# Gathering the early sums' pieces into the first step of each group of four tiles, ahead of v on ScalarE

## The chip, the cores and the metric

The kernel runs on one core of a Trainium2 chip. The metric is the time of the whole kernel on the device, in microseconds; the time before is the median of three runs. The engines work side by side and meet at semaphores: TensorE (PE), VectorE (DVE), ScalarE (ACT), GpSimd (POOL), and SyncE (SP), which here only issues transfers. In the trace every engine but PE's weight loads starts its instructions in the order of the program, so one that waits holds back all that stand behind it on its engine.

## What is computed

Sixteen sequences of 512 tokens with 128 features go through a state-space mixer and then through a layer of eight experts, two per token. The reference, cut to the second half:

```
h = _layernorm(x, axis=-1) * (1 + cb) + sb
probs, idx = jax.lax.top_k(softmax(h @ Wr + br), 2)          # two experts a token
h = _layernorm(jax.nn.relu(xt @ W1[e] + b1[e]), g1, be1)     # 512 wide, for each expert e
y = _layernorm(jax.nn.relu(h @ W2[e] + b2[e]), g2, be2)      # 128 wide
out = gate[t, e1] * y[e1, t] + gate[t, e2] * y[e2, t]
x = x + gb * out
```

## The kernel before

First the mixer runs over the 16 sequences ("batches", b), routes every token to two experts and writes the tokens' rows, sorted by expert, to DRAM. Then the expert stage runs over 135 tiles of 128 rows (EXPERT_TILES), each of one expert. It is a software pipeline: `expert_step(s)` is written once for each engine, and in step s an engine works on several tiles at once, for instance PE on the hidden layer of tile s (`hidden`, L1612 to L1614, the first instruction of a step for three tiles in four), the second layer of tile s-4 (L1725) and the transposes of tile s-2 (`turn_hidden`, L1620). A first step of a group of four (s % 4 == 0, TOGETHER = 4) begins on PE with the bias rows of four tiles (L1602).

On ACT a step is, in the order of the program: `high_part` (L799, h3hi), `hidden` (L803, relu into r), v (L906, relu of the second layer's value), `hidden_turned` (L807, the transposed hidden layer into rT), vs (L914), sde (L918, a square root). In a first step `hidden_turned` stands ahead of v; in the others behind it. DVE's step has v0 (`values`, L1398, which empties PE's value bank), the reciprocal (L1406, needs sde of the step before), vg (`scaled`, L1409, which v waits for), h3lo (L1176, which PE's next hidden layer waits for), two statistics and the target rows (L1382). POOL adds a shift to each result (L699) and scatters the rows to DRAM (L711).

The weighted sum of a token's two results is made while the expert stage runs, for the first 11 batches (EARLY). SP loads a batch's results from DRAM into early01 (`load_early`, L596, 512 KB; two buffers, the tile name is xi) and the batch is then taken in four pieces (b, j) of 128 tokens. For a piece, ACT scales the first result (`early_y0g`, L879, into a tile n), DVE adds the second result times its gate (`early_sum`, L1493), POOL multiplies by gb and adds x (L752, L758). 44 pieces are spread evenly over steps 53 to 136:

```
def piece_tile(b, j):
    return FIRST_COMBINED + (b * J + j) * (LAST_PIECE - FIRST_COMBINED) // (EARLY * J - 1)

def early_y0g(b, j):
    if j == 0:
        act.wait_ge(early_loaded[b % 2], b // 2 * 16 + 16)
```

The first piece of batches 0 to 10 falls on steps 53, 60, 68, 76, 83, 91, 99, 107, 114, 122 and 130. SP's loop is a queue of its own, ahead of the engines: its turn i loads the rows of tile i and the shifts of tile i-6, and waits for POOL's add of tile i-14 to free the shifts' buffer. The load of batch b is issued in turn piece_tile(b, 0) + 1 (LOADED_AT), behind that turn's other transfers; in a turn that opens a group of four these are six, since the biases of four tiles go ahead.

Of the kernel before, what the change touches and what calls it, by code (L numbers as in the profile page):

```python
# [6 lines left out]
def adaln_ssm_moe_kernel(nc, x_in, win_in, bin_in, bp_in, cp_in, dp_in, wout_in, bout_in, wr_in, br_in,  # L7
# [24 lines left out]
    J = L // P  # L32
# [10 lines left out]
    EXPERT_TILES = TOPK * NT + E - 1  # L43
# [24 lines left out]
    with ExitStack() as ctx:  # L68
# [51 lines left out]
        TOGETHER = 4  # L120
# [115 lines left out]
        EARLY = EXPERT_TILES // 8 + 1 - EARLY_TURN  # L236
# [12 lines left out]
        def piece_tile(b, j):  # L249

            return FIRST_COMBINED + (b * J + j) * (LAST_PIECE - FIRST_COMBINED) // (EARLY * J - 1)

        def pieces_at(i):

            return [(b, j) for b in range(EARLY) for j in range(J) if piece_tile(b, j) == i]

        assert all(tiles_for(b) + 14 <= piece_tile(b, 0) for b in range(EARLY))
        WIDE_UNTIL = 32
# [47 lines left out]
        def rows_bank(i):  # L306
            s = i - 2
            return bank[7] if s % 2 else hidden_banks[(s // TOGETHER + 1) * TOGETHER % len(hidden_banks)]
# [84 lines left out]
        def on(i, n):  # L393

            return not isinstance(i, int) or 0 <= i < n
# [21 lines left out]
        def norms(s):  # L417

            return slice(0 if on(s - 3, EXPERT_TILES) else 1, 2 if on(s - 6, EXPERT_TILES) else 1)
# [358 lines left out]
        def _(act):  # L778
# [18 lines left out]
            def high_part(i, of):  # L797
                act.wait_ge(t3_done, i + 1)
                nc.scalar.activation(h3hi[i % DEPTH], of, ACT.Copy).then_inc(h3hi_ready, 1)  # L799

            def hidden(i):
                act.wait_ge(h_done, i + 1)
                nc.scalar.activation(r[i % DEPTH], hidden_bank(i)[:], ACT.Relu).then_inc(r_ready, 1)  # L803

            def hidden_turned(i):
                act.wait_ge(tr_done, i + 1)
                nc.scalar.activation(rT[i % DEPTH], turned_bank[:], ACT.Copy).then_inc(rT_ready, 1)  # L807
# [59 lines left out]
            def half_gates():  # L867
                act.wait_ge(lead_ready, 1)
                nc.scalar.activation(gate[:, 0, :], lead[:], ACT.Tanh, scale=0.5).then_inc(half_gate_ready, 1)
                nc.scalar.activation(root_of_eps[:], eps[:], ACT.Sqrt)  # L870

            def early_y0g(b, j):
                if b == 0 and j == 0:
                    act.wait_ge(gates_ready, 1)
                if j == 0:
                    act.wait_ge(early_loaded[b % 2], b // 2 * 16 + 16)
                    if b >= 2:
                        act.wait_ge(early_sum_ready, (b - 1) * J)
                nc.scalar.activation(y0g[b % 2][:, j, :], early01[b % 2][:, j, 0:D], ACT.Copy,  # L879
                                     scale=gate[:, 0, b * J + j:b * J + j + 1]).then_inc(early_y0g_ready, 1)  # L880


            def late_y0g(b, groups):
                if groups[0] == 0:
                    act.wait_ge(late_loaded[b], 16)
                for j in groups:
                    nc.scalar.activation(late01[b][:, j, 0:D], late01[b][:, j, 0:D], ACT.Copy,  # L887
                                         scale=gate[:, 0, b * J + j:b * J + j + 1]).then_inc(early_y0g_ready, 1)

            def expert_step(s, n):  # L890
                q = n % 2
                last_of_group = s % TOGETHER == 0
                if on(s + 1, EXPERT_TILES) and s + 1 >= EARLY_H:
                    high_part(s + 1, rows_bank(s + 1)[:, 0:P])
                if s == 1:
                    half_gates()
                if on(s - 1, EXPERT_TILES) and s - 1 >= EARLY_H:
                    hidden(s - 1)
                turned_first = s >= EXPERT_TILES or last_of_group
                if on(s - 3, EXPERT_TILES) and s > 3 and turned_first:  # L900
                    hidden_turned(s - 3)
                if on(s - 5, EXPERT_TILES):
                    act.wait_ge(v0_ready, s - 4)
                    if on(s - 7, EXPERT_TILES):
                        act.wait_ge(vg_ready, s - 6)
                    nc.scalar.activation(v[1 - q][:], v0[1 - q], ACT.Relu).then_inc(v_ready, 1)  # L906
                if on(s - 3, EXPERT_TILES) and s > 3 and not turned_first:
                    hidden_turned(s - 3)
                if on(s - 8, LAST_SHIFTED):
                    act.wait_ge(vg_ready, s - 7)  # L910
                    act.wait_ge(rse_ready, s - 4)
                    if on(s - 8 - VS, EXPERT_TILES):
                        act.wait_ge(y_ready, s - 7 - VS)
                    nc.scalar.activation(vs[(s - 8) % VS], vg[q][:], ACT.Copy, scale=rse[q][:, 1:2]).then_inc(vs_ready, 1)  # L914
                if on(s - 3, EXPERT_TILES) or on(s - 6, EXPERT_TILES):
                    both = norms(s)
                    act.wait_ge(mve_ready, s - 2)
                    nc.scalar.activation(sde[q][:, both], mve[q][:, both, 1], ACT.Sqrt, bias=eps[:]).then_inc(sde_ready, 1)  # L918
                for b, j in pieces_at(s):
                    early_y0g(b, j)  # L920
                if s == EXPERT_TILES + 3:
                    late_y0g(EARLY, range(HALF))
                if s == EXPERT_TILES + 4:
                    late_y0g(EARLY, range(HALF, J))
# [27 lines left out]
        def _(dve):  # L952
# [471 lines left out]
            def hidden_norm(s, q, p):  # L1424
                dve.wait_ge(stf_ready, s - 2)
                dve.nop(nofuse=True)
                return vec.bn_aggr(mve[q][:, 0, :], stf[p][:])

            def last_step(s, n):
                q, p = n % 2, 1 - n % 2  # L1430
                if on(s - 5, EXPERT_TILES):
                    values(s, q, p)
                if on(s - 3, EXPERT_TILES):
                    hidden_norm(s, q, p)
                if on(s - 2, EXPERT_TILES):
                    hidden_stats(s - 2)
                if on(s - 6, EXPERT_TILES):
                    value_stats(s, q)
                    value_norm(s, q).then_inc(mve_ready, 1)
                reciprocals(s, p)  # L1440
                scaled(s, p)

            def expert_step(s, n):
                if s >= EXPERT_TILES:
                    last_step(s, n)
                    return
                q, p = n % 2, 1 - n % 2
                if s == TABLE2_STEPS + 1:
                    dve.wait_ge(spread_done, 2)
                    dve.wait_ge(y_done, TABLE2_STEPS - 3)  # L1450
                    write_table(bank[5], ROUND1, EXPERT_TILES)
                    dve.wait_ge(table_ready, 2)
                stats_first = s % TOGETHER == 0 and s > TOGETHER
                if stats_first:
                    hidden_norm(s, q, p)
                    hidden_stats(s - 2)
                if on(s - 5, EXPERT_TILES):
                    values(s, q, p)
                if on(s - 4, EXPERT_TILES) or on(s - 7, EXPERT_TILES):
                    reciprocals(s, p)  # L1460
                if on(s - 7, EXPERT_TILES):
                    scaled(s, p)
                if on(s + 1, EXPERT_TILES) and s + 1 >= EARLY_H:
                    low_part(s + 1, rows_bank(s + 1)[:, 0:P])
                if on(s - 6, EXPERT_TILES):
                    value_stats(s, q)
                if on(s - 3, EXPERT_TILES) and not stats_first:
                    ins = hidden_norm(s, q, p)
                if on(s - 2, EXPERT_TILES) and s > 2 and not stats_first:
                    hidden_stats(s - 2)  # L1470
                if on(s - 6, EXPERT_TILES):
                    ins = value_norm(s, q)
                if on(s - 3, EXPERT_TILES) or on(s - 6, EXPERT_TILES):
                    ins.then_inc(mve_ready, 1)
                if on(s, TABLE2_STEPS):
                    round2_table(s)
                if on(s, EXPERT_TILES):
                    target_of(s, n % SLOTS)
                for b, j in pieces_at(s - 1):
                    early_sum(b, j)  # L1480
                if isinstance(s, int) and s == 4:
                    all_gates()
# [23 lines left out]

            run_tiles(expert_step)

            for i in range(EXPERT_TILES - 1, EXPERT_TILES + 2):
                for b, j in pieces_at(i):  # L1510
                    early_sum(b, j)

# [275 lines left out]
```

## Time and profile before

| | us |
|---|---|
| median of three runs | 512.86 (512.68 to 513.87) |
| the profiled execution, its own time | 515.06 |
| its span in the trace | 513.1 |
| PE busy in the span | 487.1 |
| DVE busy | 445.1 |
| ACT busy | 412.6 |

The expert stage takes the stretch from about 175 to 500 us of the span. Times in rows are counted from the span's start; a row of the timeline gives start, duration, engine, line, operation, tiles (the tile written, then an arrow, then those read), and in brackets how long the engine had been idle before it and what ended that. The k-th L1612 of PE belongs to tile k, so the distance of two of them is the length of a step.

### The profile page before, as it was taken

How to read it: one execution, taken by the hardware profiler on the slowest of the kernel's cores; microseconds unless marked ns; L12 is line 12 of the kernel's file. 1: busy time of each engine (PE TensorE's matmuls, PEld its weight loads, DVE VectorE, ACT ScalarE, POOL GpSimd, SP SyncE). 2: the span in 40 equal slices, each digit the busy share in tenths (PEclk: the TensorE clock that was granted, in tenths of full speed). 3: DMA queues.
4: the chain of work that ended last, by engine and by line, in shares of the span. 5: the costliest groups of instructions: out<-in, count | busy, mean ns of one | idle time of the engine just before them, and what ended most of it. 6: DMA issues, size and time to landing. Idle time of an engine off the chain costs nothing. (4 is left out here: it accounts for less than half of the span.)

```text
span 513.1 us, 15015 instructions
## 1 busy us (share of the span) xinstructions
PE 487.1 (95%) x3051; PEld 372.0 (72%) x3051; DVE 445.1 (87%) x2217; ACT 412.6 (80%) x1140; POOL 360.1 (70%) x483
## 2 busy tenths in 40 slices
PE   7989999999987799999999999999999999999994
PEld 6445656555545588888888778888888888888861
DVE  7779999998887599888887789999999999999994
ACT  3679887978764588889888888898888898999984
POOL 1003666666667778888888878788787788988871
PEclk9999999999995699999999999999999999999998
DMA  6980111154111568878726686765766667666665
GB/s 167 309 240 21 46 48 46 48 130 114 52 47 55 135 151 164 161 225 198 178 89 157 178 204 162 191 194 159 208 190 145 192 208 203 175 180 207 189 177 164
DMA packets 80329, 78.36 MB, mean 153 GB/s; under 512 B 11420, under 2 KB 73015, under 8 KB 80242
## 3 DMA queue, kind: packets, MB, share of 16 engines
q1 hardware_dynamic: 71826, 60.48, 46.9%
q0 software_dynamic: 8416, 16.93, 9.3%
q8 instruction: 29, 0.48, 0.4%
q14 instruction: 58, 0.48, 0.3%
HBM read 55.20 MB, written 22.62 MB: 152 GB/s over the span
## 5 line engine op out<-in xcount | busy, mean ns | idle before, releaser
L683 POOL DMA_INDIRECT expert_rows<-rows_ring,slot x128 | 123.3, 964 | 94.5 <-issue 78.4
L711 POOL DMA_INDIRECT expert_results<-y,target x119 | 120.8, 1015 | 30.6 <-issue 24.5
L1725 PE MATMUL bank<-W,h2T 128*128 x720 | 97.4, 278 | 1.8 <-issue 0.8
L1725 PEld LDWEIGHTS bank<-W,h2T 128*128 128x128 f32 x720 | 88.2, 193 | 13.1 <-issue 6.7
L906 ACT ACTIVATE v<-wmod 128x128 f32<-128x128 f32 x135 | 41.8, 310 | 40.0 <-DVE vg L1409 35.0
L1612 PE MATMUL bank<-W1hi,h3hi 128*128 x135 | 66.6, 494 | 1.4 <-DVE h3lo L1176 1.4
L792 ACT ACTIVATE n<-X,nm,rs 128x128 f32<-128x128 f32 x128 | 54.1, 485 | 12.8 <-DVE nm L1343 12.8
L1398 DVE SCALAR_TENSOR_TENSOR wmod<-bank,rse,shifts 128x128 f32<-128x128 f32 x119 | 41.0, 344 | 24.2 <-PE bank L1725 23.3
L1181 DVE BATCH_NORM_STATS2 stf<-h1T 128x6 f32<-128x512 f32 x90 | 59.3, 659 | 0.4 <-ACT h1T L803 0.4
L1620 PE MATMUL bank<-ident_wr,h1T 128*128 128x128 f32 x360 | 55.2, 276 | 0.0
L1613 PE MATMUL bank<-W1lo,h3hi 128*128 x135 | 54.4, 403 | 0.0
L1614 PE MATMUL bank<-W1hi,h3lo 128*128 x135 | 54.2, 401 | 0.0
L803 ACT ACTIVATE h1T<-bank 128x512 f32<-128x512 f32 x90 | 53.0, 589 | 0.6 <-PE bank L1614 0.6
L807 ACT ACTIVATE h2T<-bank 128x512 f32<-128x512 f32 x90 | 52.8, 587 | 0.3 <-PE bank L1620 0.3
L1725 PE MATMUL bank<-W,third_rT 128*128 x360 | 48.1, 276 | 0.9 <-DVE wmod L1398 0.7
L1725 PEld LDWEIGHTS bank<-W,third_rT 128*128 128x128 f32 x360 | 43.7, 191 | 6.0 <-issue 2.3
L1409 DVE SCALAR_TENSOR_TENSOR vg<-v,mve,shifts 128x128 f32<-128x128 f32 x119 | 44.2, 371 | 0.0
L1620 PEld LDWEIGHTS bank<-ident_wr,h1T 128*128 128x128 f32 x360 | 42.7, 143 | 1.2 <-issue 0.4
L918 ACT ACTIVATE sde<-mve,eps 128x2 f32<-128x2 f32 (+1 forms) x138 | 40.7, 295 | 1.7 <-DVE mve L1422 0.7
L1176 DVE TENSOR_TENSOR h3lo<-bank,h3hi 128x128 fp32r<-128x128 f32 x135 | 38.0, 282 | 2.4 <-ACT h3hi L799 2.3
L799 ACT ACTIVATE h3hi<-bank 128x128 fp32r<-128x128 f32 x135 | 34.8, 260 | 4.5 <-PE bank L1593 4.5
L1417 DVE BATCH_NORM_STATS2 sty<-v 128x6 f32<-128x128 f32 x135 | 38.0, 282 | 0.2
(249 smaller groups left out, 1196.9 us busy)
## 6 DMA issues: line engine op xcount, KB each, us to landing
shifts<-expert_shifts SPq DMA_DIRECT2D x119, 192.0 KB
hrow<-expert_rows SPq DMA_DIRECT2D x135, 65.0 KB
xi<-expert_results SPq DMA_DIRECT2D x12, 512.0 KB, 5.2
out_x<-X SPq DMA_DIRECT2D x15, 256.0 KB
X<-in_L_attn_x SPq DMA_DIRECT2D x7, 512.0 KB, 7.4
b_ring<-b_two_parts SPq DMA_DIRECT2D x135, 4.0 KB
W1lo<-in_L_ffn_W SPq DMA_DIRECT2D x4, 512.0 KB, 6.7
expert_rows<-rows_ring,slot POOLq DMA_INDIRECT x128
```

The source lines that it names most:

```text
L683: nc.gpsimd.indirect_dma_start(out=rows_d, out_offset=bass.IndirectOffsetOnAxis(ap=slot[q][:, n // TOPK, n % TOPK:n % TOPK + 1], axis=0), ...
L711: nc.gpsimd.indirect_dma_start(out=results_d, out_offset=bass.IndirectOffsetOnAxis(ap=target[i % TARGETS][:], axis=0), in_=y[k], in_offset ...
L792: ins = nc.scalar.activation(dst[:, j:j + 1, :], X[:, bass.ds(b * J + j, 1), :], ACT.Identity, bias=nm_[:, x_tiles + j:x_tiles + j + 1], s ...
L803: nc.scalar.activation(r[i % DEPTH], hidden_bank(i)[:], ACT.Relu).then_inc(r_ready, 1)
L807: nc.scalar.activation(rT[i % DEPTH], turned_bank[:], ACT.Copy).then_inc(rT_ready, 1)
L1181: vec.bn_stats(stf[i % 2][:], r[i % DEPTH]).then_inc(stf_ready, 1)
L1409: vec.scalar_tensor_tensor(wide(vg[p][:]), wide(v[p][:]), mve[p][:, 1, 0:1], wide(shift_rows[ring(s - 7)][:, D:2 * D]), ALU.subtract, ALU. ...
L1612: mm(h, h3hi[i % DEPTH], W1hi[:, bass.ds(e, 1), :], start=False, stop=False)
L1613: mm(h, h3hi[i % DEPTH], W1lo[:, bass.ds(e, 1), :], start=False, stop=False)
L1614: mm(h, h3lo[i % DEPTH], W1hi[:, bass.ds(e, 1), :], start=False, stop=True).then_inc(h_done, 1)
L1620: ins = tr(turned_bank[:, ch * P:(ch + 1) * P], r[i % DEPTH][:, ch * P:(ch + 1) * P], ident[:])
L1725: ins = mm(acc, rT[(s - 4) % DEPTH][:, ch * P:(ch + 1) * P], W2[:, bass.ds(e4 * CF + ch, 1), :], start=(ch == 0), stop=(ch == CF - 1))
```

## The change

The function that tells which pieces belong to a step now takes piece_tile rounded down to a multiple of four, so that pieces go to the first step of their group: two in most groups, three in step 80, one in step 136. On ACT they stand behind `hidden_turned` and ahead of v, where before a piece stood at the end of its step. On DVE the sum of a piece stands at the end of the same step, where before it stood at the end of the next. The turns in which SP issues loads and stores still go by piece_tile itself.

```
--- before.py
+++ after.py
@@ -252,7 +252,7 @@
 
         def pieces_at(i):
 
-            return [(b, j) for b in range(EARLY) for j in range(J) if piece_tile(b, j) == i]
+            return [(b, j) for b in range(EARLY) for j in range(J) if piece_tile(b, j) // TOGETHER * TOGETHER == i]
 
         assert all(tiles_for(b) + 14 <= piece_tile(b, 0) for b in range(EARLY))
         WIDE_UNTIL = 32
@@ -899,6 +899,8 @@
                 turned_first = s >= EXPERT_TILES or last_of_group
                 if on(s - 3, EXPERT_TILES) and s > 3 and turned_first:
                     hidden_turned(s - 3)
+                for b, j in pieces_at(s):
+                    early_y0g(b, j)
                 if on(s - 5, EXPERT_TILES):
                     act.wait_ge(v0_ready, s - 4)
                     if on(s - 7, EXPERT_TILES):
@@ -916,8 +918,6 @@
                     both = norms(s)
                     act.wait_ge(mve_ready, s - 2)
                     nc.scalar.activation(sde[q][:, both], mve[q][:, both, 1], ACT.Sqrt, bias=eps[:]).then_inc(sde_ready, 1)
-                for b, j in pieces_at(s):
-                    early_y0g(b, j)
                 if s == EXPERT_TILES + 3:
                     late_y0g(EARLY, range(HALF))
                 if s == EXPERT_TILES + 4:
@@ -1476,7 +1476,7 @@
                     round2_table(s)
                 if on(s, EXPERT_TILES):
                     target_of(s, n % SLOTS)
-                for b, j in pieces_at(s - 1):
+                for b, j in pieces_at(s):
                     early_sum(b, j)
                 if isinstance(s, int) and s == 4:
                     all_gates()
@@ -1506,7 +1506,7 @@
 
             run_tiles(expert_step)
 
-            for i in range(EXPERT_TILES - 1, EXPERT_TILES + 2):
+            for i in range(EXPERT_TILES, EXPERT_TILES + 2):
                 for b, j in pieces_at(i):
                     early_sum(b, j)
```

ACT in step 80 of the expert stage; `n_1` and `n_0` are the scaled results of an odd and an even batch (here 3 and 4), and the brackets name the semaphores that a row waits for. Before:

```order
L807 ACTIVATE third_rT<-bank 128x512 [waits tr_done]
L906 ACTIVATE v<-wmod 128x128 [waits vg_ready,v0_ready]
L914 ACTIVATE wmod<-vg,rse 128x128 [waits y_ready,rse_ready,vg_ready]
L918 ACTIVATE sde<-mve,eps 128x2 [waits mve_ready]
L879 ACTIVATE n_1<-xi,gate 128x128
L799 ACTIVATE h3hi<-bank 128x128 [waits t3_done]
```

Now:

```order
L807 ACTIVATE third_rT<-bank 128x512 [waits tr_done]
L879 ACTIVATE n_1<-xi,gate 128x128 x2
L879 ACTIVATE n_0<-xi,gate 128x128 [waits early_sum_ready,early_loaded0]
L908 ACTIVATE v<-wmod 128x128 [waits vg_ready,v0_ready]
L916 ACTIVATE wmod<-vg,rse 128x128 [waits y_ready,rse_ready,vg_ready]
L920 ACTIVATE sde<-mve,eps 128x2 [waits mve_ready]
L799 ACTIVATE h3hi<-bank 128x128 [waits t3_done]
```

The first piece of batch 4, which waits for that batch's load (early_loaded0), has come from the end of step 83 to the middle of step 80, and v, vs, sde and the next step's h3hi stand behind it.

DVE at the end of step 80 and the start of step 81 (target of tile 80, then v0 of the next step). Before:

```order
L1382 TENSOR_SCALAR target<-hrow,tile_e 128x1 [waits result_stored0,hrow_loaded0]
L1398 SCALAR_TENSOR_TENSOR wmod<-bank,rse,shifts 128x128 [waits rse_ready,shifts_loaded4,y_done]
L1406 RECIPROCAL rse<-sde 128x2 [waits vs_ready,sde_ready]
L1409 SCALAR_TENSOR_TENSOR vg<-v,mve,shifts 128x128
L1176 TENSOR_TENSOR h3lo<-bank,h3hi 128x128 [waits h3hi_ready]
```

Now:

```order
L1382 TENSOR_SCALAR target<-hrow,tile_e 128x1 [waits result_stored0,hrow_loaded0]
L1493 SCALAR_TENSOR_TENSOR n_1<-xi,gate,n_1 128x128 [waits early_y0g_ready] x2
L1493 SCALAR_TENSOR_TENSOR n_0<-xi,gate,n_0 128x128 [waits early_gb_ready,early_y0g_ready]
L1398 SCALAR_TENSOR_TENSOR wmod<-bank,rse,shifts 128x128 [waits rse_ready,shifts_loaded4,y_done]
L1406 RECIPROCAL rse<-sde 128x2 [waits vs_ready,sde_ready]
```

Three sums now stand between the targets of step 80 and v0 of step 81, and the third waits for the piece of batch 4 on ACT. PE's and SP's instructions are the same rows in the same order before and now.

## Rows read from the trace of the kernel before

**Rows 1.** The page: busy time by engine, and granted clock in 40 slices

```profile
PE 487.1 (95%) x3051; PEld 372.0 (72%) x3051; DVE 445.1 (87%) x2217; ACT 412.6 (80%) x1140; POOL 360.1 (70%) x483
...
PEclk9999999999995699999999999999999999999998
```

**Rows 2.** Timeline of PE: first hidden matmul of some steps

```profile
294.92 0.48 PE L1612 MATMUL bank<-W1hi,h3hi 128*128 x1
...
310.35 0.50 PE L1612 MATMUL bank<-W1hi,h3hi 128*128 x1
...
319.55 0.50 PE L1612 MATMUL bank<-W1hi,h3hi 128*128 x1
...
356.98 0.50 PE L1612 MATMUL bank<-W1hi,h3hi 128*128 x1
...
359.14 0.48 PE L1612 MATMUL bank<-W1hi,h3hi 128*128 x1
...
378.70 0.48 PE L1612 MATMUL bank<-W1hi,h3hi 128*128 x1
...
398.30 0.48 PE L1612 MATMUL bank<-W1hi,h3hi 128*128 x1
...
417.17 0.47 PE L1612 MATMUL bank<-W1hi,h3hi 128*128 x1
...
424.20 0.50 PE L1612 MATMUL bank<-W1hi,h3hi 128*128 x1
...
454.15 0.47 PE L1612 MATMUL bank<-W1hi,h3hi 128*128 x1
```

**Rows 3.** DMA issues: KB each, median us from issue to landing

```profile
xi<-expert_results SPq DMA_DIRECT2D x12, 512.0 KB, 5.2
```

**Rows 4.** Timeline of SP's queue: loads of batches 0, 4 to 7, 9

```profile
288.80 0.39 SPq L596 DMA_DIRECT2D xi<-expert_results  x1
...
358.49 0.38 SPq L596 DMA_DIRECT2D xi<-expert_results  x1
...
376.51 0.42 SPq L596 DMA_DIRECT2D xi<-expert_results  x1
...
396.05 0.42 SPq L596 DMA_DIRECT2D xi<-expert_results  x1
...
415.36 0.38 SPq L596 DMA_DIRECT2D xi<-expert_results  x1
...
447.89 0.43 SPq L596 DMA_DIRECT2D xi<-expert_results  x1
```

**Rows 5.** Timeline, steps 96 and 97: ACT, DVE and PE

```profile
396.71 0.31 ACT L906 ACTIVATE v<-wmod 128x128 f32<-128x128 f32 x1
...
397.20 0.29 ACT L918 ACTIVATE sde<-mve,eps 128x2 f32<-128x2 f32 x1
...
398.49 0.33 DVE L1409 SCALAR_TENSOR_TENSOR vg<-v,mve,shifts 128x128 f32<-128x128 f32 x1
...
398.92 0.31 ACT L906 ACTIVATE v<-wmod 128x128 f32<-128x128 f32 x1 [0.76 <-DVE vg L1409]
...
399.13 0.58 ACT L807 ACTIVATE h2T<-bank 128x512 f32<-128x512 f32 x1
...
400.09 0.60 PE L1620 MATMUL bank<-ident_wr,decay 128*128 128x128 f32 x4
```

**Rows 6.** Groups by line, 290 to 490 us: busy us, mean ns | idle

```profile
L1493 DVE SCALAR_TENSOR_TENSOR n<-xi,gate,n 128x128 f32<-128x128 f32 x42 | 19.3, 460 | 0.0
...
L879 ACT ACTIVATE n<-xi,gate 128x128 f32<-128x128 f32 x43 | 16.7, 387 | 0.1
```

**Rows 7.** Timeline of PE, end of mixer and first expert steps

```profile
156.78 2.15 PE L1680 MATMUL bank<-ident_wr,h2T 128*128 128x136 f32 x8 [2.85 <-DVE placed L1321]
...
175.32 0.79 PE L1612 MATMUL bank<-W1hi,h3hi 128*128 x1
...
178.83 0.47 PE L1612 MATMUL bank<-W1hi,h3hi 128*128 x1
```

More of the change, by code:

```diff
@@ L253, in pieces_at @@
         def pieces_at(i):
-            return [(b, j) for b in range(EARLY) for j in range(J) if piece_tile(b, j) == i]
+            return [(b, j) for b in range(EARLY) for j in range(J) if piece_tile(b, j) // TOGETHER * TOGETHER == i]
         assert all(tiles_for(b) + 14 <= piece_tile(b, 0) for b in range(EARLY))
@@ L901, in expert_step @@
                     hidden_turned(s - 3)
+                for b, j in pieces_at(s):
+                    early_y0g(b, j)
                 if on(s - 5, EXPERT_TILES):
@@ L918, in expert_step @@
                     nc.scalar.activation(sde[q][:, both], mve[q][:, both, 1], ACT.Sqrt, bias=eps[:]).then_inc(sde_ready, 1)
-                for b, j in pieces_at(s):
-                    early_y0g(b, j)
                 if s == EXPERT_TILES + 3:
@@ L1478, in expert_step @@
                     target_of(s, n % SLOTS)
-                for b, j in pieces_at(s - 1):
+                for b, j in pieces_at(s):
                     early_sum(b, j)
@@ L1507, in _ @@
             run_tiles(expert_step)
-            for i in range(EXPERT_TILES - 1, EXPERT_TILES + 2):
+            for i in range(EXPERT_TILES, EXPERT_TILES + 2):
                 for b, j in pieces_at(i):
```

## Prediction

> **What bounds the kernel now.** I read the page first: PE is busy 95% of the span, ahead of DVE with 87% and ACT with 80% [rows 1]. So the change, which touches no matmul, can help only where PE now waits, and can hurt only where it makes PE wait. The second view is the timeline of PE, cut down to the first hidden matmul of each step: the distance of two such rows is a step, and what is more than the clean length is PE waiting for someone. The reader is to compare two stretches. From step 60 to step 64 a group of four takes 319.55 - 310.35 = 9.20 us. From step 80 to step 108, seven groups take 424.20 - 356.98 = 67.22 us, and seven clean ones would take 64.40 [rows 2]. So PE loses 2.8 us there, which is the stretch where pieces fall on the last step of a group, and ACT's piece at the end of that step holds back the relu and the copy of the group's first step. The third view is SP's own queue: when each batch's load is issued [rows 4], with the time to landing from the list of transfers, 5.2 us [rows 3]. The fourth is the timeline of all engines over a first step and the one behind it, which shows who waits for whom [rows 5].
>
> **What is moved, and what it costs by itself.** Nothing is removed: 44 pieces on ACT at 0.387 us and as many sums on DVE at 0.46 us [rows 6] stay, and so do POOL's two instructions a piece. On ACT two pieces (0.77 us) now stand ahead of v in a first step. Their cover is ACT's spare time in the next step: in step 97 it stood idle 0.76 us until vg was there [rows 5]. So I cost this at nothing; without the cover it would be up to 0.77 us in each of some 20 groups, 15 us. On DVE two sums a group stand behind one another instead of in two steps; DVE has 13% of the span free [rows 1], about 1.2 us of a group of 9.20, so a lag of one sum is made up within the group. Nothing again; without that, up to 0.46 us a group, 9 us. POOL's pairs come in two turns instead of four, and POOL is busy 70% [rows 1]: its results come late by about one piece and SP's loads with them, which I leave out of the sum. What the change is worth where it does as it says: the 2.8 us of steps 80 to 108, no more, since the groups that are clean already stay as they are.
>
> **The wait that it adds.** The first piece of a batch waits for the batch's load. SP issues that load in turn piece_tile + 1, which the change leaves alone, while the piece moves ahead by up to three steps. For batches 4, 5, 6 and 7 the first piece falls on step 83, 91, 99, 107, always the last of a group, so it moves by three: to steps 80, 88, 96, 104. Take batch 6. Issued at 396.05 [rows 4], landed 5.2 us later, at 401.25. The piece's new place is where v stood, 396.71 in step 96 [rows 5]. ACT would stand there for 4.5 us, less 0.39 for the other piece of the step. Behind it on ACT are v, vs, sde and the next step's h3hi, and on DVE the sum of that same piece waits at the end of step 96, with v0 of step 97 behind it; PE's second layer of step 97 waits for that v0, so PE stops in the step behind the first.
>
> How long after the landing (call it T) does PE go on? On ACT: the piece 0.39, then v to the start of sde 0.49 (396.71 to 397.20), sde 0.29. Then DVE's vg 0.33, then 0.10 until ACT's v of the next step starts (398.49 + 0.33 to 398.92), 0.21 from there to the copy into rT (399.13), which takes 0.58: T + 2.39 in all, and only then can PE transpose. In step 97 undisturbed, this transpose began at 400.09, 1.79 us after the step's first matmul at 398.30 [rows 2, 5]. So the loss is T - (start of the step behind the first) + 0.60. The start is in [rows 2], T is issue [rows 4] plus 5.2:
>
> Batch 4: 363.69 - 359.14 + 0.60 = 5.2. Batch 5: 381.71 - 378.70 + 0.60 = 3.6. Batch 6: 401.25 - 398.30 + 0.60 = 3.6. Batch 7: 420.56 - 417.17 + 0.60 = 4.0. Together 16.4 us. If the chain behind the landing costs nothing (the lower bound), it is 13.9.
>
> For the loads of batches 8 to 10 the piece moves by two steps at most, and the one that comes nearest is batch 9: 453.09 - 454.15 + 0.60 is below nothing, so ACT waits and PE does not. Batches 1 to 3 do not move their first piece. Batch 0 moves by one step, from 53 to 52, and step 53 is a long one already, since SP comes late there: 294.00 + 0.60, plus a mean step of 2.30 (a quarter of 9.20), against 294.92, the start of step 54 before [rows 2, 4], gives 2.0 at most and nothing at least, if the load comes sooner than the 5.2 us; I take 1.0.
>
> The gain of 2.8 us does not come in full. A load's turn is tied to POOL's results of about three steps before the piece, so where the steps between get shorter, the piece asks sooner for a load that comes no sooner, and the time turns up in the wait. I take half, 1.4; bounds 0 and 2.8.
>
> **The clock.** PE stands still for 3 to 5 us in each of the four waits. In this trace the granted clock was half of full, 1.2 GHz, in most of the 12th and 13th of the 40 slices counted from 0 [rows 1], around a place where PE had stood for 2.85 us [rows 7]. A step begun at half clock took 178.83 - 175.32 = 3.51 us [rows 7], 1.21 more than the mean 2.30. How long it would stay low after such a wait, no row of the expert stage shows. Bounds: not at all, and two steps after each of the four waits, 9.7 us. I take one step each, 4.8 us, since these waits are longer than the 2.85. The Trainium skill, TensorE: Matmul & The Clock Gate, section "What's actually happening", says that the slow clock is the default state and that only activity releases it. By that rule every one of the four waits pays, and the sum is the one below; this trace agrees as far as its one slow stretch goes.
>
> **The sum.** 16.4 + 1.0 - 1.4 + 4.8 = 20.8 us. On the profiled execution's own 515.06 this gives 535.9; that execution lies 2.2 us above the median of 512.86, so for the median 533.7, 4.1% slower.
>
> **The rivals.**
> - The waits come but the clock stays (PE has work within each wait, the next step's hidden matmuls). Then 20.8 - 4.8 = 16.0, 528.9. For it: the clock was full in slices 14 to 38 [rows 1], although PE lost time in that stretch too. Against it: these waits are longer than what it lost there in any step. Chance 0.22.
> - The waits are half as long, 514.4 to 524, because loads land sooner: SP's turns would have to come about two us earlier against the steps. For it: the waits themselves give SP time. Against it: each load's turn lies after the recovery from the last wait, and its own transfers ahead of it take their time whatever PE does. Chance 0.09.
> - The other side: the load is there when the piece asks. Then the 2.8 us of steps 80 to 108 go and nothing comes for them: 510.1, faster. It decides at one point, whether the load of batch 6 lands before 396.7 rather than at 401.25, and equally for 4, 5 and 7; it would take loads issued 5 us sooner. Against it: SP's rows are the same in the same order. Chance 0.05.
> - The change does nothing that can be measured: small waits (only ACT's, within its spare 0.76 us) and small gains, within 0.3% (1.5 us, about what a measurement of this kernel can tell from no change). It would take waits of about a microsecond where rows give three to five. Chance 0.03.
>
> **How the numbers follow.** The forecast, waits and slow clock, has 0.61. Its own range is 526 to 541: below, the chain at nothing, the gain in full and one slow step for two waits; above, the sum with two slow steps a wait and 2.0 for batch 0. With the rivals, 521 to 541 leaves out the faster case, the unchanged one and most of the half-long waits, and what is above 541. Slower by over 0.3%: 0.61 + 0.22 + 0.09 = 0.92; within 0.3%: 0.03; faster: 0.05.
>
> **What would show it.** In the profile after, ACT's group of v or of pieces gets new idle time that ends with the load from the results (the waits' list names the transfer), some 4 to 6 us each in steps 80, 88, 96 and 104, and PE's steps 81, 89, 97 and 105 are longer by 3 to 5 us, with v0 on DVE as what they wait for. Steps at a group's end elsewhere go back to clean length. The row of granted clock shows new slices under 9 between 355 and 430 us. I am wrong if the first piece of batches 4 to 7 starts right behind the copy into rT, if PE has other work while ACT waits so that the step behind it does not grow, or if the loss sits in DVE's pairs of sums, spread over all groups.

## The result and the profile after

| | us, median (lowest to highest) |
|---|---|
| before | 512.86 (512.39 to 513.94, 5 runs) |
| after | 534.71 (534.22 to 536.15, 5 runs) |
| ratio | 1.0398, 95% interval 1.037 to 1.0426 |

The change makes the kernel 21.85 us slower. The profiled execution of after took 534.56 us, with a span of 532.5, beside 515.06 and 513.1 before, so the two traces differ by 19.4 us in the span: the profiled execution of before lies 2.2 us above its median.

The page of after: busy time by engine, and the granted clock in 40 slices of 13.3 us. These answer to [rows 1].

```profile
PE 491.2 (92%) x3051; PEld 377.1 (71%) x3051; DVE 443.2 (83%) x2217; ACT 413.5 (78%) x1140; POOL 356.5 (67%) x483
...
PEclk9999999999966999999999999998989989999999
```

No engine has more instructions, and ACT and DVE have hardly more work or less (413.5 and 443.2 us here, 412.6 and 445.1 before). The shares fall because the span has grown: the new time is waiting. New slices under 9 stand in places 27, 29 and 32, counted from 0, which are 359 to 373, 386 to 399 and 426 to 439 us.

The waits of after from 280 to 510 us: who waited, for whom, us in total, how often, the longest.

```profile
ACT n L879 <- DMA xi<-expert_results: 23.9, 8, 5.2
...
DVE n L1493 <- ACT n L879: 21.0, 8, 4.8
...
PE bank L1725 <- DVE wmod L1398: 16.8, 9, 4.3
```

Read downwards, the long waits of these lines are four events, each seen from three engines: ACT's piece waits for the load, DVE's sum waits for the piece, and PE's second layer waits for v0 (L1398), which stands behind that sum on DVE. Each is a little shorter on the next engine, since that engine has a little work left before it stops. Of ACT's 23.9 us, 18.7 are the four; the rest is batch 0 (2.33 us) and the loads of batches 8 to 10 (2.9 us together).

The timeline of after around the four places (start, duration, what, and in brackets the idle time before it and who ended it):

```profile
356.87 0.38 SPq L596 DMA_DIRECT2D xi<-expert_results  x1
...
357.68 0.48 PE L1612 MATMUL bank<-W1hi,h3hi 128*128 x1
...
361.70 0.40 ACT L879 ACTIVATE n<-xi,gate 128x128 f32<-128x128 f32 x1 [5.02 <-DMA xi<-expert_results]
...
362.14 0.35 DVE L1493 SCALAR_TENSOR_TENSOR n<-xi,gate,n 128x128 f32<-128x128 f32 x1 [4.70 <-ACT n L879]
...
362.41 0.34 DVE L1398 SCALAR_TENSOR_TENSOR wmod<-bank,rse,shifts 128x128 f32<-128x128 f32 x1
...
363.01 1.90 PE L1725 MATMUL bank<-W,third_rT 128*128 x8 [4.27 <-DVE wmod L1398]
...
364.70 1.06 PE L1620 MATMUL bank<-ident_wr,h1T 128*128 128x128 f32 x4
...
365.42 0.78 PE L1612 MATMUL bank<-W1hi,h3hi 128*128 x1
...
368.11 0.48 PE L1612 MATMUL bank<-W1hi,h3hi 128*128 x1
...
382.37 0.48 PE L1612 MATMUL bank<-W1hi,h3hi 128*128 x1
...
385.35 0.40 ACT L879 ACTIVATE n<-xi,gate 128x128 f32<-128x128 f32 x1 [4.27 <-DMA xi<-expert_results]
...
391.79 0.49 PE L1612 MATMUL bank<-W1hi,h3hi 128*128 x1
...
405.98 0.48 PE L1612 MATMUL bank<-W1hi,h3hi 128*128 x1
...
409.85 0.40 ACT L879 ACTIVATE n<-xi,gate 128x128 f32<-128x128 f32 x1 [5.16 <-DMA xi<-expert_results]
...
416.19 0.48 PE L1612 MATMUL bank<-W1hi,h3hi 128*128 x1
...
430.36 0.47 PE L1612 MATMUL bank<-W1hi,h3hi 128*128 x1
...
433.32 0.40 ACT L879 ACTIVATE n<-xi,gate 128x128 f32<-128x128 f32 x1 [4.25 <-DMA xi<-expert_results]
...
439.76 0.48 PE L1612 MATMUL bank<-W1hi,h3hi 128*128 x1
```

Steps 81 and 82 run from 357.68 to 368.11, 10.43 us; before they took 4.28. PE had done its part of step 81 at 358.7 and then had nothing until 363.01. The pattern comes back three times, and the second, third and fourth can be read from three rows each: the start of the step behind the piece, the piece, and the start two steps on.

The windows of after in two of the four places: the wait, then the stretch behind it (us, busy time by engine, granted clock, DMA share, GB/s).

```profile
357.70:363.00 5.30, 1.04 (x7) 0.59 (x4) 0.79 (x4) 1.30 (x6) 0.31 (x1) 1.00 0.62 202
363.30:366.70 3.40, 3.40 (x15) 3.15 (x15) 3.03 (x15) 3.09 (x10) 2.75 (x4) 0.51 0.38 113
...
406.00:411.10 5.10, 1.04 (x7) 0.59 (x4) 0.75 (x4) 1.25 (x6) 0.27 (x1) 0.99 0.63 194
411.10:414.50 3.40, 3.34 (x14) 3.25 (x15) 2.86 (x15) 2.92 (x9) 1.62 (x3) 0.51 0.34 105
```

PE works for 1.04 us of the 5.3 of the wait, at a granted clock of 1.00, and then for the whole 3.4 us behind it at 0.51, that is nearly all at 1.2 instead of 2.4 GHz. All four places show this and no other between 300 and 490 us does. The third does not show in the page's row of the clock: it lies across the border of slices 30 and 31, so that neither drops below 9.

**The difference by stretch.** Taking the first hidden matmul of each step (L1612) in both traces and subtracting step lengths gives where the time sits, in us against before. The runs of the next section stand beside it. "The eight steps" are 81, 82, 89, 90, 97, 98, 105 and 106.

| kernel | up to step 3 | 3-50 | 51-56 | 57-80 | the eight steps | other steps 81-107 | 108-133 | sum |
|---|---|---|---|---|---|---|---|---|
| after | -1.3 | -0.1 | -0.3 | +0.2 | **+22.2** | -2.3 | +1.2 | +19.6 |
| load_one_turn_sooner | -1.0 | +0.3 | +1.9 | 0.0 | **+3.7** | -2.1 | 0.0 | +2.8 |
| load_three_turns_sooner | -0.7 | +0.1 | +1.9 | -0.1 | **+0.2** | -2.2 | +0.1 | -0.7 |
| round_up | -0.4 | +1.2 | +1.0 | 0.0 | **-0.2** | -1.2 | +0.1 | +0.5 |
| round_up_load0_later | +0.5 | +0.1 | -1.5 | +0.1 | **-0.2** | -2.1 | +0.1 | -2.9 |
| grouping_alone | -1.1 | +1.8 | -0.2 | +1.3 | **+20.7** | -1.2 | +1.1 | +22.3 |
| sum_one_step_later | +0.2 | +0.6 | +2.4 | +1.4 | **+23.1** | -1.3 | +1.3 | +27.8 |
| busy_in_wait | -1.1 | +0.2 | +1.6 | 0.0 | **+22.6** | -2.5 | +0.2 | +21.1 |
| busy_in_wait_12 | -1.2 | -0.1 | -0.2 | -0.1 | **+21.6** | -1.8 | +0.2 | +18.3 |

No piece lies ahead of step 52, so the first two columns are not the change's: they show how far two executions differ there anyway, up to 1.8 us. The change is in the eight steps.

### The profile page after: what moved, and what is told of

It reads as the page before. It is cut to its first block and busy times, and to the rows that moved or that the text cites. A ratio compares the mean times of both kernels' runs of the same rounds, so it can differ in the third digit from the quotient of the medians.

```text
span 532.5 us, 15015 instructions
## 1 busy us (share of the span) xinstructions
PE 491.2 (92%) x3051; PEld 377.1 (71%) x3051; DVE 443.2 (83%) x2217; ACT 413.5 (78%) x1140; POOL 356.5 (67%) x483
## 5 line engine op out<-in xcount | busy, mean ns | idle before, releaser
L1725 PEld LDWEIGHTS bank<-W,h2T 128*128 128x128 f32 x720 | 88.8, 194 | 19.4 <-issue 12.0
L1612 PE MATMUL bank<-W1hi,h3hi 128*128 x135 | 67.9, 503 | 0.7 <-DVE h3lo L1176 0.7
L1398 DVE SCALAR_TENSOR_TENSOR wmod<-bank,rse,shifts 128x128 f32<-128x128 f32 x119 | 41.1, 345 | 24.8 <-PE bank L1725 21.7
L1725 PE MATMUL bank<-W,third_rT 128*128 x360 | 49.7, 283 | 9.1 <-DVE wmod L1398 8.6
L1725 PEld LDWEIGHTS bank<-W,third_rT 128*128 128x128 f32 x360 | 45.0, 197 | 14.6 <-issue 11.3
L699 POOL TENSOR_TENSOR y<-wmod,shifts 128x128 f32<-128x128 f32 x58 | 27.5, 475 | 27.5 <-ACT wmod L916 26.8
L1409 DVE SCALAR_TENSOR_TENSOR vg<-v,mve,shifts 128x128 f32<-128x128 f32 x119 | 45.4, 382 | 0.0
L1593 PE MATMUL bank<-ident_wr,hrow 128*128 128x128 f32 x135 | 37.1, 277 | 1.6 <-DMA hrow<-expert_rows 1.6
```

Source lines behind the costliest of these rows:

```text
L1409: vec.scalar_tensor_tensor(wide(vg[p][:]), wide(v[p][:]), mve[p][:, 1, 0:1], wide(shift_rows[ring(s - 7)][:, D:2 * D]), ALU.subtract, ALU. ...
L1612: mm(h, h3hi[i % DEPTH], W1hi[:, bass.ds(e, 1), :], start=False, stop=False)
L1725: ins = mm(acc, rT[(s - 4) % DEPTH][:, ch * P:(ch + 1) * P], W2[:, bass.ds(e4 * CF + ch, 1), :], start=(ch == 0), stop=(ch == CF - 1))
```

## The experiments

The theory: the piece is asked for three steps before the turn at which SP issues its load has been moved, so the load is late, four times. The rivals: the place ahead of v, or the two sums in one step of DVE, cost something by themselves; and the clock has no share in it. Each kernel is the kernel after with the edit shown, except where it says otherwise. The kernel before ran on the same chip each time: 515.19 us (513.01 to 516.58, 17 runs) beside load_one_turn_sooner, round_up, grouping_alone and busy_in_wait, and 513.61 (511.83 to 515.33, 23 runs) beside the other four.

**load_one_turn_sooner.** The loads of all batches but the first are issued one turn earlier; nothing else moves.

```
-            LOADED_AT = {piece_tile(b, 0) + 1: b for b in range(EARLY)}
+            LOADED_AT = {piece_tile(b, 0) + (b == 0): b for b in range(EARLY)}
```

> The changed kernel, with the loads of batches 1 to 10 issued one turn of SP's queue sooner (turn piece_tile instead of piece_tile + 1; batch 0 stays); pieces, sums and their places as changed. Theory (the whole loss is the wait for loads that were not moved, and the slow clock that follows): for batches 4 to 7 this turn lies ahead of the row numbers and the four bias transfers that open a group, so the load goes out some 4.5 us sooner, which is about what ACT waited (4.3 to 5.2 us); the waits are gone or under 1 us, the clock stays full, 510.5 to 514. Rival (the new place costs by itself: two pieces ahead of v on ACT, two sums behind one another on DVE): little changes, above 528.

519.31 us (517.42 to 521.33), ratio 1.0087 [1.0057, 1.0116]. Its timeline, the four pieces that wait:

```profile
354.46 0.39 SPq L596 DMA_DIRECT2D xi<-expert_results  x1
...
361.19 0.40 ACT L879 ACTIVATE n<-xi,gate 128x128 f32<-128x128 f32 x1 [1.86 <-DMA xi<-expert_results]
...
379.73 0.40 ACT L879 ACTIVATE n<-xi,gate 128x128 f32<-128x128 f32 x1 [0.50 <-DMA xi<-expert_results]
...
399.24 0.41 ACT L879 ACTIVATE n<-xi,gate 128x128 f32<-128x128 f32 x1 [1.37 <-DMA xi<-expert_results]
...
419.04 0.41 ACT L879 ACTIVATE n<-xi,gate 128x128 f32<-128x128 f32 x1 [1.41 <-DMA xi<-expert_results]
```

One line of SP's table, and 18.5 of the 22.2 us in the eight steps are gone. ACT waited 18.7 us for the four loads in after and 5.1 here, which is 13.6 less; the other 4.9 go to the clock, which stood at 1.00 in the stretch behind each of these short waits (the section on the prediction puts its price in after at 5.1). The load is still late by 0.5 to 1.9 us, since it took longer to land than reckoned: 361.19 - 354.46 = 6.7 us for batch 4, and 5.5 to 6.6 for the others. Therefore it does not beat before, and the expected total is missed.

**load_three_turns_sooner.** The same by three turns, as far as the piece itself had moved.

```
-            LOADED_AT = {piece_tile(b, 0) + 1: b for b in range(EARLY)}
+            LOADED_AT = {piece_tile(b, 0) + (1 if b == 0 else -2): b for b in range(EARLY)}
```

> The changed kernel, with the loads of batches 1 to 10 issued three turns of SP's queue sooner, as far as the pieces of batches 4 to 7 moved; batch 0 stays. One turn sooner left ACT waiting 1.9, 0.5, 1.4 and 1.4 us in the four steps, and PE some 3.7 us in all. Theory: no wait for these loads, so 3.7 us less than with one turn, ratio 0.993 to 1.004, with batch 0's wait (up to 3 us) as what is left. Rival (one turn sooner left something else than waits): 1.006 to 1.011 as there.

513.56 us (512.18 to 516.12), ratio 1.0008 [0.9992, 1.0025]: as before, as expected. Its waits on ACT from 300 to 490 us:

```profile
ACT v L908 <- DVE vg L1409: 15.9, 38, 1.5
ACT v L908 <- DVE wmod L1398: 0.7, 1, 0.7
ACT v L908 <- issue: 0.3, 1, 0.3
```

The wait for the load is no longer among them. This kernel has the change whole, with its place on ACT and its sums on DVE, and is not slower: the place costs nothing that shows (-0.1 us in steps 57 to 80, where no load is waited for). In the profiled execution the 2.2 us that the change was to gain in steps 83 to 107 are there, and nearly all were taken back by batch 0, whose load was left where it was (+1.9 in steps 51 to 56).

**round_up.** The pieces go to the first step of the next group instead of that of their own.

```
-            return [(b, j) for b in range(EARLY) for j in range(J) if piece_tile(b, j) // TOGETHER * TOGETHER == i]
+            return [(b, j) for b in range(EARLY) for j in range(J) if -(-piece_tile(b, j) // TOGETHER) * TOGETHER == i]
```

> The changed kernel, with piece_tile rounded up to a multiple of four instead of down: still grouped in first steps, ahead of v, the sum in the same step, but no piece asks for its load sooner than before; SP's queue as before. Theory: no wait for loads, the gain at the ends of groups stays: 509.5 to 513. Rival (place and pairs cost by themselves): above 528.

513.53 us (511.48 to 516.05), ratio 0.9973 [0.9955, 0.9991]: faster than before by 0.3%, and half a microsecond above the expected range. So small a gain stays uncertain: the median of before itself lies between 512.86 and 515.19 us over the three sets of runs, and the profiled execution of round_up was no shorter than that of before (+0.5 in the table). It is the same edit moved later, where every load has landed. Its timeline, steps 53 to 55:

```profile
291.88 0.48 PE L1612 MATMUL bank<-W1hi,h3hi 128*128 x1
...
294.45 0.33 PE L1593 MATMUL bank<-ident_wr,hrow 128*128 128x128 f32 x1 [1.62 <-DMA hrow<-expert_rows]
...
296.36 0.48 PE L1612 MATMUL bank<-W1hi,h3hi 128*128 x1
...
298.50 0.47 PE L1612 MATMUL bank<-W1hi,h3hi 128*128 x1
...
300.42 0.33 PE L1593 MATMUL bank<-ident_wr,hrow 128*128 128x128 f32 x1 [0.97 <-DMA hrow<-expert_rows]
...
303.00 0.51 PE L1612 MATMUL bank<-W1hi,h3hi 128*128 x1
```

No piece waits here, but steps 53 and 55 are long all the same (296.36 - 291.88 = 4.48, 303.00 - 298.50 = 4.50): PE waits for the rows of the tile, which SP loads behind the load of batch 0.

**round_up_load0_later.** Round_up, with batch 0's load two turns later, to free those rows.

```
-            LOADED_AT = {piece_tile(b, 0) + 1: b for b in range(EARLY)}
+            LOADED_AT = {piece_tile(b, 0) + (3 if b == 0 else 1): b for b in range(EARLY)}
```

> Rounding up, which beat the kernel before, with batch 0's load two turns later (its first piece stands in step 56 there). In round_up SP stood before that load until the first results were stored, and the rows of tiles 55 and 57 came late: steps 53 and 55 took 4.5 us each. Theory: these rows come in time, 2 to 4 us less than round_up, ratio 0.989 to 0.995. Rival (the rows are late for another reason): as round_up, 0.995 to 0.999.

512.77 us (511.64 to 516.12), ratio 0.9987 [0.997, 1.0005]. In the profile step 53 fell from 4.48 to 2.15 us and step 55 from 4.50 to 3.49, while step 51 rose by 0.79 against before; over steps 51 to 56 it is 2.5 us less than round_up (-1.5 against +1.0 in the table). In the runs the expected 2 to 4 us are not there: by its ratio this kernel can't be told apart from before, and it lies no lower than round_up's. So batch 0's load explains step 53 and part of step 55 in the profile; that moving it is worth anything in the median is not shown.

**grouping_alone.** The kernel before, with only the grouping: pieces stay at the end of ACT's step, sums stay a step later.

```
-            return [(b, j) for b in range(EARLY) for j in range(J) if piece_tile(b, j) == i]
+            return [(b, j) for b in range(EARLY) for j in range(J) if piece_tile(b, j) // TOGETHER * TOGETHER == i]
```

> The kernel before, with only the rounding down to the first step of a group; on ACT the pieces stay at the end of their step, on DVE the sums stay one step later. Theory: the same four loads are waited for, at the end of the first step; v and sde of that step are out by then and DVE is not held, so each wait costs PE some 0.7 us less, and less of the slow clock: 526 to 533. Rival (the place ahead of v and the sums in the same step cost): about as before, 511 to 515.

538.8 us (537.76 to 539.68), ratio 1.0467 [1.0435, 1.0499]. Its timeline, the starts of steps 62 and 63, where no load is waited for, and the place of batch 4:

```profile
315.37 0.48 PE L1612 MATMUL bank<-W1hi,h3hi 128*128 x1
...
317.76 0.48 PE L1612 MATMUL bank<-W1hi,h3hi 128*128 x1
...
365.14 0.40 ACT L879 ACTIVATE n<-xi,gate 128x128 f32<-128x128 f32 x1 [4.65 <-DMA xi<-expert_results]
...
367.02 1.07 PE L1620 MATMUL bank<-ident_wr,h1T 128*128 128x128 f32 x4 [4.15 <-ACT h2T L807]
```

The grouping alone brings the whole loss, 20.7 us in the eight steps, although no piece stands ahead of v. PE stops at another instruction, the transposes, which wait for ACT's copy into rT: the wait reaches PE through ACT's own order. So the loss is neither the place nor DVE's sum. From the piece to the start two steps on it took 6.0 us in all four places, 0.4 less than in after, where 0.7 less was expected. The total is 5.8 us above what was expected. Before itself was 2.3 us longer beside these runs (515.19 against 512.86), and the rest is a second cost: step 62 took 317.76 - 315.37 = 2.39 us, 0.25 more than before, and ten of the 17 groups from step 60 on show 0.25 to 0.27 in this same step, the third of the group. By the table, the steps outside the eight and behind step 56 are 1.4 + 1.0 + 1.0 = 3.4 us longer than in load_three_turns_sooner, where no load is waited for either.

**sum_one_step_later.** After, with DVE's sums back in the step behind the piece.

```
-                for b, j in pieces_at(s):
+                for b, j in pieces_at(s - 1):
                     early_sum(b, j)
```

> The changed kernel, with DVE's sums put back to the end of the next step; ACT as changed. It asks through which of the two chains the wait reaches PE. Theory (ACT's own order is enough: v, sde and the next step's copy into rT stand behind the waiting piece): PE stops at the transposes instead of the second layer and loses about as much, ratio 1.034 to 1.044. Rival (it is DVE's sum in the same step that hands the wait on): the loss falls to less than half, under 1.02.

542.78 us (541.48 to 545.5), ratio 1.0573 [1.054, 1.0605]: the slowest of all, and above what the theory expected, so that the total is missed. Its waits from 300 to 490 us:

```profile
ACT n L879 <- DMA xi<-expert_results: 19.7, 6, 5.1
...
DVE rse L1406 <- ACT sde L920: 16.7, 4, 4.5
PE bank L1620 <- ACT h2T L807: 11.4, 3, 4.2
```

Without the sum in its way, DVE waits for sde, which stands behind the piece on ACT, and PE for the copy into rT (the fourth wait, 4.27 us, is listed under that copy's other buffer, third_rT). The sum was one of two ways by which the wait reached PE; with it taken away the other carries all, and the eight steps lose 23.1 us. And the extra 0.26 us a group are back: nine of 17 groups show 0.25 to 0.29 in their third step, and after shows none in any of these. Both kernels that have DVE's two sums in a group's second step show them, and in each of the seven others at most one group has such a value. Reckoned as above they are 1.5 + 0.9 + 1.2 = 3.6 us here, so the change's move of the sums into the first step is worth some 3.5 us against a grouping without it. A further 2.7 us against after lie in steps 51 to 56, where the clock fell behind batch 0's wait.

**busy_in_wait and busy_in_wait_12.** After, with 24 (12) small matmuls of zeros on PE ahead of its wait for v0, in steps 81, 89, 97 and 105. They add zero to a bank that PE fills next, so they only keep PE at work.

```
+                    if s in (81, 89, 97, 105):
+                        for _ in range(24):
+                            mm(hidden_bank(s + 1)[0:64, 0:P], ident[0:64, 64:128], ident[0:64, :], start=False, stop=False)
                     if on(s - 5, EXPERT_TILES):
                         pe.wait_ge(v0_ready, s - 4)
```

> The changed kernel, with 24 matmuls of a quarter of a zero matrix put on PE in steps 81, 89, 97 and 105, ahead of the wait that holds it (they add zero to a bank that is not yet in use, so nothing of the result changes); about 3 us of work in waits of 3.3 to 4.3 us. Theory (waits of some 16 us and slow clock of some 5): the granted clock stays full in all four, the waits on ACT stay as long, 528.5 to 531.5. Rival (the slow clock lies within time that is lost anyway): 533.5 to 535.

535.49 us (534.77 to 535.77), ratio 1.0392 [1.0361, 1.0424]: the expected total is missed. The clock stayed full behind all four waits, but the 24 matmuls took some 5.4 us, longer than the waits, and held PE themselves. On the price of the clock this says nothing.

> As busy_in_wait, with 12 matmuls instead of 24: 24 took 5.4 us, longer than the waits, so that they held PE past their end. 12 should take 2.7 us and end inside each wait. Theory (the slow clock behind each wait costs 1.6 us, read from the run of the changed kernel as 5.1 us from the second layer of the step to the start of the next step but one, against 3.5 at full clock): clock full in all four, ratio to before 1.025 to 1.032, some 6 us less than the changed kernel. Rival (the slow clock lies within lost time): 1.037 to 1.043, as the changed kernel.

533.89 us (531.46 to 537.78), ratio 1.0401 [1.0364, 1.0439]: no different from after. The expected total is missed, and the ratio lies where the rival put it. The total alone would thus speak for the rival; the single waits speak against it. The timeline of PE and ACT in the second one:

```profile
383.15 2.83 PE L1721 MATMUL bank<-ident_wr 64*64 64x128 f32 x24
...
385.58 0.40 ACT L879 ACTIVATE n<-xi,gate 128x128 f32<-128x128 f32 x1 [4.71 <-DMA xi<-expert_results]
...
386.78 1.15 PE L1728 MATMUL bank<-W,h2T 128*128 x8 [0.80 <-DVE wmod L1398]
...
387.47 0.58 ACT L807 ACTIVATE third_rT<-bank 128x512 f32<-128x512 f32 x1
...
388.19 0.63 PE L1620 MATMUL bank<-ident_wr,h1T 128*128 128x128 f32 x4 [0.26 <-ACT third_rT L807]
...
390.72 0.48 PE L1612 MATMUL bank<-W1hi,h3hi 128*128 x1
```

The windows behind the first, second and fourth wait (columns as above; the granted clock is the third number from the end):

```profile
363.50:366.90 3.40, 3.40 (x15) 2.83 (x14) 2.91 (x14) 3.13 (x11) 2.96 (x5) 0.50 0.44 124
387.00:390.40 3.40, 3.14 (x25) 2.79 (x25) 3.38 (x16) 3.40 (x11) 2.58 (x5) 1.00 0.36 105
435.20:438.60 3.40, 3.40 (x14) 3.00 (x15) 2.10 (x11) 3.03 (x10) 2.83 (x6) 0.51 0.58 154
```

In the second and third wait the clock held, and the eight matmuls of the second layer took 1.15 us where after has 1.7 to 2.1 in its four. From the piece to the start two steps on it took 390.72 - 385.58 (ACT's piece) = 5.14 us, and 5.14 again in the third. In the first and fourth, where the loads came later and PE still stood for 1.5 and 2.2 us behind the added matmuls, the clock fell and it took 6.37 and 6.75. The waits themselves differ from those of after by up to 1.9 us (ACT waited 5.13, 4.71, 4.39 and 6.11 us, where after has 5.02, 4.27, 5.16 and 4.25). Together they are 1.6 us longer, which hides most of what two saved slow stretches give back.

## Why the prediction was right

The mechanism, the places and the size held: ACT's piece waits for the load in the four places that were named, PE stops in the step behind, on v0 from DVE, and the clock falls behind each wait. The median was forecast at 533.7 us and came at 534.71. The sum on the profiled execution's own time was 535.9 against 534.56. That it came so close is in part luck, since terms missed by about a microsecond each and offset one another: the chain by +0.9 and steps 108 to 133 by +1.2, the gain by -0.9 and batch 0 by -1.3. By its terms:

**The waits.** The prediction put T - (start of the step behind the first) at 13.9 us in all. In after it is 361.70 - 357.68 = 4.02, then 385.35 - 382.37 = 2.98, 409.85 - 405.98 = 3.87 and 433.32 - 430.36 = 2.96, together 13.83. Single ones missed by up to 0.9 us, as the load landed 4.8 to 5.7 us after its issue and not 5.2 each time. With the chain of 0.60 a wait the unrounded terms give 16.3 and not 16.4, which changes nothing.

**The chain behind the landing** was mis-sized. From the piece to the start two steps on, after took 6.41, 6.44, 6.34 and 6.44 us, 25.63 in all, partly at half clock. At full clock this way is 5.14 us in the two waits of busy_in_wait_12 where the clock held, and 5.14 to 5.25 in the four of load_one_turn_sooner. Before, the eight steps took 17.29 us. So the chain costs 4 x 5.14 - 17.29 = 3.3 us, where 4 x 0.60 = 2.4 was put. The way was the right one, and its length was short: the prediction let PE transpose 2.39 us behind the landing, and in the second wait of busy_in_wait_12 the transposes start 388.19 - 385.58 = 2.61 us behind the piece, released by the copy into rT as foreseen. Four times this 0.22 is the 0.9 us that was missed. The copy began 1.89 us behind the piece (387.47) where 1.81 was put, and between its end at 388.05 and the transposes lie 0.14 us that the sum left out.

**The clock** costs 25.63 - 4 x 5.14 = 5.1 us, 1.27 for each wait; 1.21 was put, read from one of the expert stage's first steps [rows 7]. That step itself gives nearly the same price when it is compared with its like: step 4 took 3.51 us before, at half clock, and 175.34 - 173.18 = 2.16 us in after, at full clock, which is 1.35. The argument for one slow step a wait was weaker. It went by the wait of 2.85 us at the mixer's end, but that wait began at 153.93, and the clock had fallen by 154.40 (granted 1.00 from 150.00 to 154.30, 0.50 from 154.40 to 157.00), so it cannot be what this wait brought about. That each of the four waits then paid about one slow step was a guess that came true, not something that the row showed. The three terms give 13.8 + 3.3 + 5.1 = 22.2, which is what the eight steps grew by. The rival that the clock stays full is thus refuted by the trace, and busy_in_wait_12 shows the price as a difference between waits of one run. The Trainium skill, TensorE: Matmul & The Clock Gate, section "What's actually happening", calls the slow clock the default, which activity releases. The trace agrees as far as it goes: in all four places the clock fell behind a wait of PE (0.51 over the next 3.4 us) and was back at 1.00 after those 3.4 us in which PE worked almost throughout.

**The gain** was undersized: 1.4 us was put, half of 2.8, since shorter steps were to show up again as longer waits. Steps 83 to 107 outside the eight gained 2.3 us, and the waits did not grow by it (13.83 against 13.9). The halving was wrong: 2.3 of the 2.8 came.

**Batch 0** was put at 1.0 with bounds 0 and 2.0. In after it shows -0.3 us in steps 51 to 56. But it differs between executions: five kernels keep this batch's pieces and load as in after (after, load_one_turn_sooner, load_three_turns_sooner, busy_in_wait, busy_in_wait_12), and their profiles give -0.3, 1.9, 1.9, 1.6 and -0.2. Their mean is 1.0 by chance, for there are two kinds. In the three high ones the granted clock fell to half behind this wait, for 3.4 us from about 295.5 on; in the two low ones it stayed full. A window of load_three_turns_sooner (columns as above):

```profile
295.00:300.00 5.00, 4.61 (x24) 4.06 (x23) 3.21 (x16) 3.74 (x11) 3.47 (x5) 0.66 0.96 143
```

The same window of busy_in_wait_12:

```profile
295.00:300.00 5.00, 5.00 (x39) 4.18 (x38) 4.81 (x23) 4.87 (x15) 3.97 (x6) 1.00 0.97 186
```

ACT's wait does not tell the two apart, 3.42 us in the first and 3.41 in the second. Steps 53 and 54 do: 5.59 and 3.54 us in the first, 4.95 and 2.14 in the second. So the slow clock makes most of the spread, 1.4 us of it in step 54 alone, and a term for it was missing here. Why the clock fell in three of these executions and not in the other two was not tried.

**What was left out.** Steps 108 to 133 grew by 1.2 us. ACT waited there for the loads of batches 8 to 10, 0.79, 0.82 and 1.26 us at 453, 472 and 491 us, where the prediction expected a wait on ACT alone that PE does not see. PE did see some of it: the steps behind these, 113, 121 and 129, grew by 0.17, 0.34 and 0.82 us. In busy_in_wait_12 the same stretch shows 0.2 in all.

**The other rivals.** "The load is there when the piece asks" did not come. It was to take loads issued 5 us sooner, which was a little short. Against the start of the step behind the piece, load_one_turn_sooner issued the four loads 3.3 to 5.1 us sooner than after, and the pieces still waited 0.5 to 1.9 us, so that by these figures 4.7 to 6.9 us were needed. Load_three_turns_sooner issued them 6.9 to 9.5 us sooner; there no piece waits, and the gain in steps 83 to 107 shows (-2.2 us). "The waits are half as long" would have needed SP's turns two us earlier in after, and they were not: the waits came as long as forecast. The 3.3 to 5.1 us of load_one_turn_sooner cut the waits to between a tenth and two fifths. The sums in pairs on DVE, as a cost spread over all groups, are excluded: after shows +0.2 us over steps 57 to 80, and only the kernels with the sums a step later show 0.26 a group.

Open are what decides whether the clock falls behind a wait such as batch 0's, and whether a version with both round_up and a better turn for batch 0's load beats before by more than the 0.3% of round_up.

## What to carry to other kernels

When a consumer moves ahead in an engine's order, its load's turn must move with it. Compare the issue plus the longest landing that the trace shows with the new place, for each batch: here a move by three steps cost 22 us in the four places, and one line of the load table gave back 18.5 of them. A wait in the middle of an in-order engine's step can reach the bounding engine by each path that leaves that engine, so moving one of the dependants need not shorten it: without DVE's sum in its way the loss here was 23.1 us instead of 22.2. When PE is made to stand for 3 to 4 us in an otherwise dense stretch, reckon with more than the wait itself: here it was 1.3 us of slow clock and 0.8 us of chain for each of the four.

## What the hardware showed that was not expected

- In after the clock was still granted at 1.00 through nearly the whole of PE's four waits of 3.26 to 4.27 us. It fell within 0.4 us of PE's return, and stayed at 1.2 GHz for 3.4 us. The matmuls that pay are those behind the wait: the eight of the second layer took 1.7 to 2.1 us instead of 1.15. In sum_one_step_later one such stretch was twice as long (0.50 from 393.5 to 400.1 us).
- In busy_in_wait_12 the clock held in the two waits where PE stood idle for 0.8 us or less behind the 2.83 us of added matmuls, and fell in the two where it stood for 1.5 and 2.2 us. These are four waits of one execution, and batch 0's wait shows that waits alike on ACT can end with either clock, so this is no rule yet.
- A matmul of 64x64 by 64x128 in f32 stands as two records in the trace, 0.118 us each (24 in 2.83 us for 12 instructions).
- The eight loads of 512 KB that a piece waited for in the four places of after and load_one_turn_sooner landed between 4.8 and 6.7 us after their issue (read at the start of the piece), and one that no piece waited for, batch 3's in after, took 7.9. So a turn taken back by a median of 5.2 left up to 1.9 us of wait.
